# Residual rows from GpSimd and an addition on VectorE in place of four products with the identity

## The reference

```python
emb = silu(sin_emb(timestep)) @ W_ada + b_ada            # one row of 512 for each entry
scale, shift = split(emb[:, None, :], 2, axis=-1)
x = ln(src) * (1.0 + scale) + shift
q, k, v = x @ Wq + bq, x @ Wk + bk, x @ Wv + bv          # 16 heads of 16
scores = einsum('bhqd,bhkd->bhqk', q / sqrt(16), k) + attention_bias
probs = softmax(where(src_mask, -inf, scores))
ctx = einsum('bhqk,bhkd->bhqd', probs, v)
x = x + (ctx @ Wo + bo)
h = ln(x) * g2 + beta2
return x + gelu2(h @ W1 + b1) @ W2 + b2
```

## Time and profile before

| | |
|---|---|
| three runs, median (lowest to highest) | 1425.97 us (1422.19 to 1427.66) |
| the profiled execution, its own time | 1427.18 us |
| its span, first to last instruction | 1425.4 us |
| mean granted TensorE clock | 0.976 of full speed |
| busy: TensorE, VectorE, ScalarE, GpSimd | 1276.8, 988.0, 903.1, 665.1 us |

### The profile page before, as it was taken

How to read it: one execution, slowest core, us unless ns; L and a number is a source line. 1 busy time by engine, 2 the same in 40 slices (tenths; PEclk the granted TensorE clock), 3 DMA queues, 4 the chain that set the end, 5 groups by cost and what they waited for, 6 DMA issues and landing times. The chain is left out here.

```text
span 1425.4 us, 34480 instructions
## 1 busy us (share of the span) xinstructions
PE 1276.8 (90%) x9923; PEld 1160.8 (81%) x9923; DVE 988.0 (69%) x2764; ACT 903.1 (63%) x2319; POOL 665.1 (47%) x580
## 2 busy tenths in 40 slices
PE   5884899999999999945899999999999999999996
PEld 4774899999999999944587888778877878788885
DVE  5776688889878987743776667566766667666652
ACT  3442677778777877722566676666666666667671
POOL 2775577787778777743032332332232232231221
PEclk9999999999999999976899999999999999999997
DMA  5885121121112111128766656655675556654620
GB/s 189 271 274 187 46 66 46 57 61 51 57 48 65 54 56 58 49 89 253 225 214 184 190 182 198 205 181 162 195 220 182 177 179 204 199 189 148 202 72 15
DMA packets 184707, 203.18 MB, mean 143 GB/s; under 512 B 18176, under 2 KB 172736, under 8 KB 184576
## 3 DMA queue, kind: packets, MB, share of 16 engines
q1 hardware_dynamic: 169136, 161.57, 36.9%
q10 hardware_dynamic: 9264, 23.47, 5.1%
q0 software_dynamic: 6176, 16.79, 3.4%
HBM read 155.89 MB, written 41.68 MB: 139 GB/s over the span
## 5 line engine op out<-in xcount | busy, mean ns | idle before, releaser
L1254 ACT ACTIVATE bias<-bias,neg_max 128x256 f32<-128x256 f32 x512 | 255.4, 501 | 193.7 <-DVE neg_max L1586 191.6
L343 POOL TENSOR_TENSOR w_lo<-w,w_hi 128x512 fp32r<-128x512 f32 x156 | 242.2, 1572 | 0.0
L1586 DVE CUSTOM_DVE_ANT_0 bias<-ps_s,bias 128x256 f32<-128x256 f32 x512 | 194.5, 417 | 34.0 <-PE ps_s L1351 21.4
L745 DVE TENSOR_TENSOR w_lo<-w,w_hi 128x512 fp32r<-128x512 f32 x156 | 149.8, 999 | 68.7 <-ACT w_hi L423 67.0
L544 PE MATMUL ps_y<-w_hi,hidT_hi 128*128 128x256 f32 x624 | 180.2, 289 | 1.9 <-DVE token_rows L759 1.9
L531 PE MATMUL ps_h<-htokT_hi,w_hi 128*128 128x256 f32 x624 | 178.5, 286 | 3.2 <-DVE htokT_lo L750 3.2
L531 PE MATMUL ps_h<-htokT_lo,w_hi 128*128 128x256 f32 x624 | 178.2, 286 | 0.0
L531 PE MATMUL ps_h<-htokT_hi,w_lo 128*128 128x256 f32 x624 | 178.1, 285 | 0.0
L1349 PE MATMUL ps_s<-mask_f,minus_ident 128*128 128x256 f32 x512 | 154.3, 323 | 25.6 <-DVE neg_max L1586 15.8
L544 PE MATMUL ps_y<-w_lo,hidT_hi 128*128 128x256 f32 x624 | 177.0, 284 | 0.0
L544 PE MATMUL ps_y<-w_hi,hidT_lo 128*128 128x256 f32 x624 | 177.0, 284 | 0.0
(11 more groups left out here) (276 smaller groups left out, 3496.9 us busy)
## 6 DMA issues: line engine op xcount, KB each, us to landing
bias<-bias_dram SPq DMA_DIRECT2D x128, 512.0 KB, 4.2
w<-w_dram ACTq DMA_DIRECT2D x32, 512.0 KB
xin<-dispatch SPq DMA_DIRECT2D x39, 256.0 KB, 2.8
expert_out<-token_rows SPq DMA_DIRECT2D x39, 256.0 KB, 2.2
q_stack<-q_hi_rows SPq DMA_DIRECT2D x64, 128.0 KB, 2.9
q_stack<-q_lo_rows SPq DMA_DIRECT2D x64, 128.0 KB, 2.9
k_stack<-k_hi_rows SPq DMA_DIRECT2D x60, 128.0 KB, 2.8
k_stack<-k_lo_rows SPq DMA_DIRECT2D x60, 128.0 KB, 2.8
```

Source lines behind the costliest of these rows:

```text
L343: pool.tensor_tensor(w2_part["lo"][:, k, :], w2_piece(e, k), w2_part["hi"][:, k, :].bitcast(F32), ALU.subtract).then_inc(sem("w2_split"), 1)
L745: dve.tensor_tensor(w1_part["lo"][:, k, :], w1_piece(e, k), w1_part["hi"][:, k, :].bitcast(F32), ALU.subtract).then_inc(sem("w1_split"), 1)
L1254: act.activation(head_rows(h, j), head_rows(h, j), ACT.Exp, scale=-1.0, bias=neg_max[par][:, h, j:j + 1], accum_out=total[par][:, h, j:j + ...
L1586: dve.tensor_tensor_reduce(head_rows(h, j), ps_s[h % 2][:, j * T:(j + 1) * T], head_rows(h, j), -1.0, LARGEST, ALU.add, ALU.min, neg_max[p ...
```

## The change

Instead of xmT the normalised rows xn (tokens on partitions) are modulated a second time, by GpSimd, with the entry's scale and shift as rows that are repeated over the partitions. VectorE then adds these rows to the projection in the operation that added the bias before. The bias of the output projection is folded into the shift row. So these parts change:

- `output` has no products with the identity, and SyncE no copy xmT_kept. SyncE loads one row of 512 numbers for each entry, repeated over 128 partitions (`load_mod`), from a table in memory.
- GpSimd gets `keep_rows`: a product and a sum over 128 x 512, the sum after a wait for the product. It stands between `prepare_sum` and `take_mask`.
- VectorE's `residual` reads `xm_rows` instead of the bias and waits for it as well; `normalise` waits until the rows of the entry before are made.
- In the routing stage TensorE makes the table by two more products, VectorE adds biases in three more operations, and SyncE loads two rows of biases and sends the table to memory.

```diff
@@ first stage, SyncE
+        sp.dma_start(cond["ada_row"], io["ada_row"].partition_broadcast(B)).then_inc(sem("ada_rows_in"), 16)
+        sp.dma_start(cond["bo_row"], io["rows"][1].partition_broadcast(B)).then_inc(sem("ada_rows_in"), 16)
         for b in range(2, B):
+            if b == 8:
+                sp.wait_ge(sem("mod_rows_ready"), 2)
+                sp.dma_start(io["mod_rows"], cond["rows"]).then_inc(sem("mod_sent"), 16)
@@ first stage, ScalarE, step
             if b == 14:
                 act.wait_ge(sem("cond_product"), 6)
+                act.wait_ge(sem("mod_sent"), 16)
@@ wave_tensor
+    for c in range(C):
+        pe.matmul(ps_a[0:B, 0:2 * D], w["wave"][:, c, :], w["ada_w"][:, c, :], start=(c == 0), stop=(c == C - 1))
     for m in range(2 * C):
@@ modulation_vector
     dve.wait_ge(sem("cond_product"), 6)
+    dve.wait_ge(sem("ada_rows_in"), 32)
+    dve.tensor_tensor(w["rows"], ps_a[0:B, 0:2 * D], w["ada_row"], ALU.add).then_inc(sem("rows_summed"), 1)
     for c in range(C):
...
+    dve.wait_ge(sem("rows_summed"), 1)
+    dve.tensor_scalar(w["rows"][:, 0:D], w["rows"][:, 0:D], 1.0, None, ALU.add).then_inc(sem("mod_rows_ready"), 1)
+    dve.tensor_tensor(w["rows"][:, D:2 * D], w["rows"][:, D:2 * D], w["bo_row"], ALU.add).then_inc(sem("mod_rows_ready"), 1)
@@ transformer, SyncE
-        def keep_rows(n, par):
-
-            sp.wait_ge(sem("xmT_ready"), C * (n + 1))
-            wait_free(sp, sem("wo_done"), n - 1, alone=True)
-            sp.dma_start(xmT_kept[par][:], xmT[:]).then_inc(sem("xm_kept"), 16)
+        def load_mod(n):
+
+            wait_free(sp, sem("xm_rows_ready"), n, alone=True)
+            sp.dma_start(mod_rows[:].rearrange("p i d -> p (i d)"), io["mod_rows"][bass.ds(n, 1), :].rearrange("b d -> (b d)").partition_broadcast(P)
+                         ).then_inc(sem("mod_in"), 16)
@@ transformer, GpSimd
+        def keep_rows(n, par):
+
+            pool.wait_ge(sem("xn2_ready"), J * (n + 1))
+            pool.wait_ge(sem("mod_in"), 16 * (n + 1))
+            pool.tensor_tensor(xm_rows[par][:], xn[:], spread(mod_rows[:, 0, :], [P, J, D], 1), ALU.mult).then_inc(sem("xm_scaled"), 1)
+            wait_alone(pool, sem("xm_scaled"), n + 1)
+            pool.tensor_tensor(xm_rows[par][:], xm_rows[par][:], spread(mod_rows[:, 1, :], [P, J, D], 1), ALU.add).then_inc(sem("xm_rows_ready"), 1)
...
                 prepare_sum(n - 1)
             if exists(n + 1):
+                keep_rows(n + 1, 1 - par)
                 take_mask(n + 1, 1 - par)
@@ transformer, ScalarE, modulate
-            wait_free(act, sem("xm_kept"), 16 * n)
@@ transformer, TensorE, output
-            pe.wait_ge(sem("xm_kept"), 16 * (n + 1))
             for j in range(J):
                 for m in range(C):
                     sums = ps_out[:, j * D + m * P:j * D + (m + 1) * P]
                     for c in range(C):
-                        pe.matmul(sums, ctxT[:, c, j * P:(j + 1) * P], wo[:, c, m * P:(m + 1) * P], start=(c == 0), stop=False)
-                    last = pe.matmul(sums, xmT_kept[par][:, m, j * P:(j + 1) * P], ident, start=False, stop=True)
+                        last = pe.matmul(sums, ctxT[:, c, j * P:(j + 1) * P], wo[:, c, m * P:(m + 1) * P], start=(c == 0), stop=(c == C - 1))
@@ transformer, VectorE
         def normalise(n):
             dve.wait_ge(sem("rstd_ready"), n + 1)
+            wait_free(dve, sem("xm_rows_ready"), n)
...
-        def residual(n):
+        def residual(n, par):
             dve.wait_ge(sem("wo_done"), n + 1)
+            dve.wait_ge(sem("xm_rows_ready"), n + 1)
...
-            dve.tensor_tensor(x3[:], halves(ps_out[:, :]), spread(bo[:], [P, J, D], 1), ALU.add).then_inc(sem("x3_ready"), 1)
+            dve.tensor_tensor(x3[:], halves(ps_out[:, :]), xm_rows[par][:], ALU.add).then_inc(sem("x3_ready"), 1)
```

More of the change, by code:

```diff
@@ L505, in _ @@
             if b == 3:
-                wave_tensor(pe, cond, ps_h1, sem)
+                wave_tensor(pe, cond, ps_h0, ps_h1, sem)
             step(b)
@@ L687, in _ @@
         step(3)
-        modulation_vector(dve, cond, vec, ps_h1, keep, sem)
+        modulation_vector(dve, cond, vec, ps_h0, ps_h1, keep, sem)
         for b in range(4, B + 2):
@@ L828, in cond_weights @@
         "hyp_w1": place(SE, 1536, SH), "hyp_w2": place(SH, 1664, SH), "sty_w1": place(SH, 1792, SH // 2),
+        "rows": more[0:B, 512:1024], "ada_row": more[0:B, 1024:1536], "bo_row": more[0:B, 1536:1792],
         "a1": sb("a1", [SH, B]), "a2": sb("a2", [SH, B]), "a3": sb("a3", [SH // 2, B]),
@@ L852, in style_tensor, with wave_tensor @@
     last.then_inc(sem("cond_product"), 1)
-def wave_tensor(pe, w, ps_b, sem):
+def wave_tensor(pe, w, ps_a, ps_b, sem):
     pe.wait_ge(sem("wave_ready"), 1)
     pe.wait_ge(sem("ada_in"), 16)
+    for c in range(C):
+        pe.matmul(ps_a[0:B, 0:2 * D], w["wave"][:, c, :], w["ada_w"][:, c, :], start=(c == 0), stop=(c == C - 1))
     for m in range(2 * C):
@@ L947, in wave_vector, with modulation_vector @@
     dve.tensor_tensor(w["wave"][:], w["half"][:], w["turns"][:], ALU.mult).then_inc(sem("wave_ready"), 1)
-def modulation_vector(dve, w, vec, ps_b, keep, sem):
+def modulation_vector(dve, w, vec, ps_a, ps_b, keep, sem):
     dve.wait_ge(sem("cond_product"), 6)
+    dve.wait_ge(sem("ada_rows_in"), 32)
+    dve.tensor_tensor(w["rows"], ps_a[0:B, 0:2 * D], w["ada_row"], ALU.add).then_inc(sem("rows_summed"), 1)
     for c in range(C):
@@ L1010, in transformer @@
     w2 = {n: sb(f"ff2_{n}", [P, F, D], F32R) for n in ("hi", "lo")}
-    bv, bo, b2 = [sb(n, [P, D]) for n in ("bv", "bo", "b2")]
+    bv, b2 = [sb(n, [P, D]) for n in ("bv", "b2")]
     q_b = sb("q_b", [P, C])
@@ L1023, in transformer @@
     xmT = sb("xmT", [P, C, T])
-    xmT_kept = [sb(f"xmT_kept{i}", [P, C, T]) for i in range(2)]
+    mod_rows = sb("mod_rows", [P, 2, D])
+    xm_rows = [sb(f"xm_rows{i}", [P, J, D]) for i in range(2)]
     part = {n: sb(n, [P, C, T], F32R) for n in ("q_hi", "q_lo", "k_hi", "k_lo")}
@@ L1152, in step @@
                     load_bias(n + 1, 0)
-                keep_rows(n + 1, 1 - par)
+                load_mod(n + 1)
                 if starting:
@@ L1240, in load_layer @@
                 act.dma_start(dst, io["ff_b1"][i * 512:(i + 1) * 512].partition_broadcast(P)).then_inc(sem("fold_in"), 16)
-            for i, dst in enumerate((bo, b2)):
-                act.dma_start(dst[:], io["rows"][1 + i].partition_broadcast(P)).then_inc(sem("layer_in"), 16)
+            act.dma_start(b2[:], io["rows"][2].partition_broadcast(P)).then_inc(sem("layer_in"), 16)
             act.dma_start(wo[:], io["wo"]).then_inc(sem("layer_in"), 16)
@@ L1410, in turn_x, with output @@
             last.then_inc(sem("xnT2_done"), 1)
-        def output(n, par):
+        def output(n):
             pe.wait_ge(sem("ctxT_ready"), n + 1)
-            pe.wait_ge(sem("xm_kept"), 16 * (n + 1))
             for j in range(J):
@@ L1503, in step @@
                 if isinstance(n, int) and n == 1 and h == 3:
-                    pe.wait_ge(sem("layer_in"), 16 * 3)
+                    pe.wait_ge(sem("layer_in"), 16 * 2)
                 if isinstance(n, int) and n == 1 and h == 7:
@@ L1514, in step @@
                     if h == 3:
-                        output(n - 1, 1 - par)
+                        output(n - 1)
                 if exists(n + 1):
@@ L1757, in step @@
                     if h == 4:
-                        residual(n - 1)
+                        residual(n - 1, 1 - par)
                         moments(n - 1)
@@ L1821, in layers @@
         io["expert_out"] = nc.dram_tensor("expert_out", (TILES * TOK, D), F32, kind="Internal").ap()
+        io["mod_rows"] = nc.dram_tensor("mod_rows_dram", (B, 2 * D), F32, kind="Internal").ap()
         for name in ("q_hi", "q_lo", "k_hi", "k_lo"):
@@ L1880 @@
         "ff_w1": chunks(second("W1")), "ff_w2": chunks(second("W2")),
-        "ff_b1": second("b1"),
+        "ff_b1": second("b1"), "ada_row": second("b_ada"),
         "rows": np.stack([second("bv"), second("bo"), second("b2")]),
```

## The result

The changed kernel takes 1437.67 us in the median of four runs (1435.78 to 1439.01), the kernel before 1425.89 in four runs beside them (1422.19 to 1427.66). The ratio is 1.0085, with a 95% interval of 1.0062 to 1.0109: it is slower, by 0.6 to 1.1%. The profiled execution took 1436.92 us and has a span of 1435.1 us, 9.7 us more than the 1425.4 us before.

A forecast was written before the change was run, and what follows sets the result against it. TensorE was taken to bound steady steps from the feed-forward to the next head 1, a VectorE-ScalarE chain the rest. Terms -2.6 + 9.8 + 3.1 = +10.3 us gave a median of 1436.3 us, eight-in-ten range 1425 to 1441.

The forecast's parts named there:

- The total: Whole kernel: +10.3 us on the profiled execution, 1436.3 us for the median, +0.7%; this forecast had a 55% chance.
- Identity products, 0 in steps 1 to 14: TensorE's output projection: removal gains nothing in steps 1 to 14, 0.9 us in step 15, 1.7 in step 16; together -2.6.
- GpSimd's product holds the second h_rows, 0.7 us in 14 steps: VectorE's second normalisation: its second operation waits for GpSimd's added product, 0.7 us later in each of 14 steps, +9.8 us.
- its first rival: Second h_rows gets in beside GpSimd's product as beside the mask conversion: no change, +0.5 us, 1426.5 us; 17%.
- The chain behind it: After the late h_rows: v_pad, head 7's minimum, exponentials, hT_hi and the feed-forward on TensorE, all without slack.
- Each step 0.7 us longer: Sign to look for in steps 1 to 14: every step lengthens by 0.7 us.
- its stretch from the feed-forward on unchanged: Sign to look for in steady steps: TensorE's part from the feed-forward on keeps its length.
- Routing stage, +3.1 us: Routing, once: two added TensorE products cost 1.7 us, three added VectorE operations 1.4 us; bounds 0 and 3.8.
- The second h_rows slips in: Rival for VectorE's second normalisation: GpSimd's product lets it through with 0.3 us, as mask_f did; +0.5 us, 1426.5 us; 17%.
- The products pay: Rival: the output products' end sets what follows in each step, so 12.6 us more go; -12.1 us, 1413.9 us; 10%.
- Both operations hold: Rival: h_rows waits for GpSimd's product and sum, 2.0 us in each of 14 steps; +28.5 us, 1454.5 us; 8%.

The follow-up runs named there:

- the one-input operation: Changed kernel with GpSimd's product replaced by a multiplication of the same values by a constant, one tensor as input: 1424.38 us, ratio 0.9997 to the kernel before.
- the halves: Changed kernel with GpSimd's product made in two operations of 256 values instead of one of 512: 1427.28 us, ratio 1.0007 to the kernel before.
- The second pair of profiles: The kernel before and the changed kernel, both unchanged, profiled once more: 1426.89 and 1440.67 us, one run each.
- the two kernels with the products: Changed kernel with four identity products an entry put back, 1436.76 us, and the same with GpSimd's mask conversion ahead of the residual rows, 1427.33 us.

## Why the prediction was right, point by point

**The total** (1436.3 us; measured 1437.67) and the sign were right, for the main reason given, but two deviations of some 5 us that cancel stand behind the close number, so its closeness is in part luck.

**Identity products, 0 in steps 1 to 14.** Right: x3 waits for nothing, and a steady step is 45.95 us with the products and 45.97 without. Their time went where the prediction put it, into TensorE's idle time. Step 15 gave 0.88 us (forecast 0.9), where x3's wait fell from 1.66 to 0.77 us. The tail behind the start of step 16 shrank by 2.2 us (forecast 1.7), so in this pair the term is mis-sized by some 0.5 us. In other pairs of profiles, with and without the products, it is 1.1 to 1.9 us.

**GpSimd's product holds the second h_rows, 0.7 us in 14 steps.** Right in mechanism, place and size: the pair takes 2.66 us (2.6 to 2.8 forecast), 1.68 in step 15, and the sum holds nothing. Exchanging the two GpSimd calls moves the turned h rows by 9.9 us over 14 steps (9.8 with the products in both), against a forecast of 9.8. That product and mask conversion differ, on which the forecast rested against its first rival, is their number of inputs: shown by the one-input operation. That the held operation gets in at the next border is shown by the halves. Between the first two profiles only 4.8 us of this appear, because that execution of the kernel before had lost some 0.6 us in each even step at ScalarE's wait for the probabilities of head 2, and this one of the changed kernel had not. The second pair of profiles, in which both have it, shows 7.4 us. What causes that wait is open.

**The chain behind it.** The prediction looked for TensorE's extra 0.7 us ahead of the feed-forward or of the scores of head 9. It stood one place earlier, ahead of the turned h rows (0.74 us); TensorE had been just in time there before. "Each step 0.7 us longer" failed as a statement: the steps of the first pair of profiles are longer by 0.06 to 1.8 us.

**Not foreseen: TensorE's lower clock level.** The step that failed is "its stretch from the feed-forward on unchanged". Some 3.4 us run at 1.2 GHz in 11 of 14 steps. In length the stretch is unchanged within 0.1 us in eight steps, five of them with a slow stretch, and longer by 0.6 to 1.0 us in six. It costs 5.3 us in the first pair of profiles, 4.7 in the second and 2.3 between the two kernels with the products. The count goes with the length of the pair in these twelve executions, and so with how long TensorE stands idle ahead of turn_h: 10 or 11 steps at 2.66 us, 0 to 4 at about 2 us, none at 0.73, whether the products are there or not. That the hold makes it frequent is shown by the exchange of two calls (11 to 3, and with the products 10 to 4). What decides in a single step, and why equal pairs give 0, 1, 3 or 4, is open. The count in the two profiles of the kernel before may be low for it. Of its 46 runs in the two groups, the 11 with a mean granted clock of 0.976 or 0.977 took 1420.3 to 1423.3 us, and the 35 at 0.971 to 0.975 took 1423.5 to 1428.7. So stretches at the lower level come and go from run to run in that kernel too. Where in the kernel they lie, no trace shows. (The first profile, at 0.976, took 1427.18 us, with the late context described above.)

The Trainium skill ("TensorE: Matmul & The Clock Gate", its part on the HAM clock gate) says that TensorE's clock is gated by how busy it has been and that the same kernel can see it differently from run to run. The counts above, 0 and 1 for one program, and the 46 runs agree.

**Routing stage, +3.1 us.** The start of the expert tiles moved by 2.2 us in the profiled execution, 1.0 of it on TensorE instead of 1.7 (rank_base waits 2.99 us; 3.7 was forecast) and 1.2 on VectorE instead of 1.4. The rows' product is longer than forecast (3.2 us for 1.7: each of its four instructions takes nearly twice as long as the two at the fold that the forecast was made from the earlier trace rows, as TensorE is slow there until it speeds up) and the sixteen instructions behind it are shorter by 1.5, when TensorE has sped up. Where it does not, the part costs 5 us, above the forecast's upper bound of 3.8. As a middle value 3.1 is fair; the reason for it was not.

**The rivals.** "The second h_rows slips in" needs a one-input operation. "The products pay" needs x3 to wait for them. "Both operations hold" would need a pair of 4 us. None of the three was here. A better version than both was in reach of the same argument, and the prediction didn't draw it: x3b itself held the first h_rows for 0.95 us in the kernel before. One wait on GpSimd makes that kernel 1.5% faster (1402.77 us). With it the change still shows no gain (1405.10 us): 2.6 us won in the last two steps, 2 to 5 lost in the routing.

## What to carry to other kernels

In this kernel a GpSimd operation with two tensors as inputs, placed beside a VectorE operation from SBUF to SBUF, costs VectorE the rest of the GpSimd operation. Look for such pairs on the path first, and move GpSimd's work behind VectorE's, or make it one-input, before taking work from TensorE where TensorE waits anyway. And a stall of 0.7 us in front of a TensorE that is otherwise full may be paid twice, since its clock can fall behind it. Count the steps with a granted clock below 1.00 in both traces, and then compare the lengths of the part that TensorE sets: a slow stretch that lies beside TensorE's waits costs nothing, as in five of eleven steps here.

## What the runs showed of the hardware that I had not expected

- The same VectorE pair (128x256 float32, two operations) takes 0.73 us with GpSimd idle, 1.68 with a two-input operation beside it, 1.99 with that and a one-input operation of 1.5 us, 2.66 with two two-input operations one after the other. The Trainium skill ("SBUF — State Buffer", Who interferes with whom) has the shared ports locked for a whole instruction and the other engine fully blocked; by that the one-input operation should have held the pair as the product did. The measured 0.31 us decides: it slows the pair and does not hold it.
- Stretches of some 3.4 us at half clock appear behind idle times of 1 us and less (0.74 and 0.78 in step 7), in an engine that is busy for 89% of the span.
- The granted clock on record for the routing stage says little about its speed. Its mean between 60 and 130 us is 1.00 in the kernel before and 0.50 in the changed one, and the time from one entry to the next there is 6.7 us in both, with the same group of matmuls 0.61 us long in both (rows of before, then after). The Trainium skill ("TensorE: Matmul & The Clock Gate", Seeing it yourself) warns that such events can be unreliable in a trace; the first two rows below agree with it. In the steady steps record and durations fit together (0.50 and 0.41 us, 1.00 and 0.28 us).

```profile
60.00:130.00 70.00, 55.34 (x245) 49.48 (x244) 50.92 (x343) 27.78 (x60) 53.82 (x53) 1.00 0.74 241
60.00:130.00 70.00, 56.32 (x251) 50.44 (x250) 51.73 (x345) 28.60 (x62) 53.15 (x53) 0.50 0.77 245
```
```profile
74.75 0.61 PE L472 MATMUL ps_h<-picked,const 128*128 128x16 f32 x2 [1.38 <-DVE picked L627]
...
77.05 0.61 PE L478 MATMUL ps_h<-picked,const 128*128 128x16 f32 x2 [1.25 <-DVE picked L633]
```
